# Last two groups of each attention program: all scores of a key tile are issued ahead of the values of the tile before

## The chip, the cores and the metric

The kernel runs on one core of a Trainium2 chip. The metric is the device time of one execution in microseconds. The engines are named as in the profile: PE (TensorE matmuls), PEld (its weight loads), DVE (VectorE), ACT (ScalarE), POOL (GpSimd) and SP (SyncE, which issues DMAs).

## The reference, cut to what matters

A decoder of six blocks, each followed by a residual sum and a layer norm: causal self attention, cross attention to a context of 1024 rows, a soft mixture of experts, causal self attention, cross attention, and a block that holds a causal self attention and a top-2 mixture of experts. Batch 4, 512 rows, width 256, 16 heads of 16. Attention is

```python
w = jnp.einsum('bhnd,bhmd->bhnm', q, k) * jax.lax.rsqrt(float(D))
w = jax.nn.softmax(w, axis=-1)          # causal in self attention
attn = jnp.einsum('bhnm,bhmd->bhnd', w, v)
```

## The kernel before

The five attentions are built as two programs, `first` (self attention a0, then cross attention c0) and `second` (a1, c1, then a2). The soft mixture of experts stands between them and the routed one behind the second. Stages are separated by a barrier of all engines.

An attention program works on groups: one batch and four of its heads. Program `first` has 32 groups (0 to 31), `second` 48 (0 to 47). A group of cross attention has 8 key tiles of 128 keys and all 512 queries; a group of self attention has 4 key tiles, and tile t takes only queries from 128·t on (widths 512, 384, 256, 128). The last two groups are thus cross attention in `first` (30, 31) and causal in `second` (46, 47).

What a group goes through:

- `unit`: scores with queries on the partitions, only to get each row's maximum (DVE). The units of group n+2 are shared out over the steps of group n. The last two groups of a program therefore have none to issue: these are the groups "without maximum scores".
- `chain`: six small DVE steps that split the maximum into three bf16 rows; `shift`: four small matmuls (L1254) and an ACT copy (L1368) that bring it to `shift_T`. Chain and shift of group n+1 happen within group n.
- `scores (t, p)`: scores with keys on the partitions, for key tile t and two of the four heads (p is 0 or 1). PE: two products (L1213), four small mask products in a causal group (L1219), two products that add the shift (L1223). Each fills two PSUM banks. ACT then takes two exponentials (L1357) into `probs`.
- `values t`: PE multiplies tile t's `probs` with `v_aug` into PSUM bank 6 (L1235). It waits for the exponentials of (t, 1). `probs` has two buffers, so ACT's exponentials of tile t wait for the values of tile t-2.
- `drain`: ACT copies bank 6 to `o_sum` when a group's last values are in (L1364); the next group's `values 0` waits for it. `turn`: PE transposes `o_sum` (L1245), DVE normalises it (L1477, L1480).

The order of work is one list, `plan`, written by `attention_plan`. Every engine walks the same list and does the events that are its own, so the order of events in the list is the order of instructions on each engine. The plan's events take PSUM banks in turn out of seven (`SHARED_BANKS`), two for a `scores`; an event may start when the reader of the event seven banks before has read (`wait_bank`). In groups 30, 31, 46 and 47 the plan holds no other products, loads or stores: only scores, values, and one turn, one drain, one `v_aug` addition and, in the first of the two, six chain steps and one shift.

Before the change a step of every group is: scores (t, 0), values t-1, scores (t, 1). In step 0 the last values and the drain of the group before take the place of values t-1; in step 1 the turn follows the values; in the last step the shift comes just ahead of scores (t, 1).

Of the kernel before, what the change touches and what calls it, by code (L numbers as in the profile page):

```python
# [726 lines left out]
def attention_plan(layers, pieces, contexts):  # L727

    slots = [layer for layer in layers for _ in range(BATCH)]
    groups = GROUPS * len(slots)
    plan = []

    def layer_of(n):
        return slots[n // GROUPS]

    def share(stream, done, total):  # L740

        while stream and stream[0][1] * total < done * stream[0][2]:
            plan.append(stream.pop(0)[0])

    def stream_of(events):

        whole, at, out = sum(cost for _, cost in events) or 1, 0, []
        for event, cost in events:
            out.append((event, at, whole))
            at += cost  # L750
        return out

    def body(n):
        units, own = [], [(x, COST.get(x[0], 300)) for x in pieces.get(n, ())]
        if 0 <= n + 2 < groups:
            units = stream_of([(("unit", n + 2, u), 1) for u in range(len(layer_of(n + 2).units))])
        if n < 0:
            plan.extend(x for x, _ in own)
            if n == -1:
                plan.extend([("augment", 0, 0), ("vload", 2, 0)])  # L760
                for k in range(SHIFT_STEPS):
                    plan.append(("chain", 0, k))
                    share(units, k + 1, SHIFT_STEPS)
                plan.append(("shift", 0, 0))
            plan.extend(x[0] for x in units)
            return
        if n == groups:
            last = layer_of(n - 1).key_tiles - 1
            plan.extend([("values", n - 1, last), ("drain", n - 1, 0), ("turn", n - 1, 0)])
            plan.extend(x for x, _ in own)  # L770
            return
        layer, own = layer_of(n), stream_of(own)
        steps = layer.key_tiles
        for t in range(steps):
            plan.append(("scores", n, (t, 0)))
            share(units, 2 * t + 1, 2 * steps)
            if t:
                plan.append(("values", n, t - 1))
            elif n:
                plan.extend([("values", n - 1, layer_of(n - 1).key_tiles - 1), ("drain", n - 1, 0)])  # L780
            if t == 1:
                if n:
                    plan.append(("turn", n - 1, 0))
                if n + 1 < groups:
                    plan.append(("augment", n + 1, 0))
                if n + 3 < groups:
                    plan.append(("vload", n + 3, 0))
                if NB <= n + 3 < groups:
                    plan.append(("load", n + 3, 0))
            if t == steps - 1 and n + 1 < groups:  # L790
                plan.append(("shift", n + 1, 0))
            plan.append(("scores", n, (t, 1)))
            share(units, 2 * t + 2, 2 * steps)
            if n + 1 < groups and t < 3:
                plan.extend([("chain", n + 1, 2 * t), ("chain", n + 1, 2 * t + 1)])
            share(own, t + 1, steps)
        assert not units and not own

    for n in range(-3, groups + 1):
        for event in contexts.get(n, ()):  # L800
            plan.append(event)
        body(n)
    return slots, plan
# [1540 lines left out]
```

How the kernel before makes its waits and increments, by code:

```python
def wait_for(eng, sem, count):  # L50
    if isinstance(count, int) and count <= 0:
        return
    eng.wait_ge(sem, count)
# [70 lines left out]
        @block.gpsimd  # L125
        def _(pool):
            for t in (c.ident, c.ident_bf, c.mask_qk, tri_kq):
                pool.memset(t[:, :], 0.0).then_inc(filled, 1)
            pool.memset(chosen[:, :, :], 0.0).then_inc(filled, 1)
            pool.memset(c.eps[:, :], LN_EPS).then_inc(c.made, 1)
            pool.wait_ge(filled, 5)
            for t in (c.ident, c.ident_bf):
                pool.affine_select(out=t[:, :], in_=t[:, :], compare_op=ALU.not_equal, fill=1.0, base=0,
                                   pattern=[[-1, P]], channel_multiplier=1).then_inc(c.made, 1)
# [3 lines left out]
                               base=0, pattern=[[1, P]], channel_multiplier=-1).then_inc(c.made, 1)  # L138
            for i in range(6):
                if i:
                    pool.wait_ge(filled, 5 + 2 * i)
                for p in range(2):
                    pool.affine_select(out=chosen[:, p, :], in_=chosen[:, p, :], compare_op=ALU.not_equal, fill=1.0,
# [3 lines left out]
        @block.vector  # L149
        def _(v):
            v.wait_ge(c.made, 5)
            for dst, src in ((c.pick, c.ident_bf), (c.mask_kq, tri_kq)):
                for own in (slice(0, 64), slice(64, P)):
                    for x in range(2):
# [1 line left out]
            v.wait_ge(filled, 17)  # L156
            v.tensor_copy(c.choose[:, :, :], chosen[:, :, :]).then_inc(c.made, 1)
            v.wait_ge(c.made, CONSTANTS)
```

## Time and profile before

| | |
|---|---|
| time, median of 3 | 2954.07 us (2953.14 to 2954.84) |
| the profiled execution's own time | 2954.8 us |
| its span | 2953.1 us |
| PE busy | 2536.9 us (86%) |
| ACT busy | 1340.6 us (45%) |
| DVE busy | 1502.1 us (51%) |
| groups 30 and 31, from values to values | 24.12 and 23.80 us |
| groups 46 and 47 | 10.92 and 11.07 us |
| mean granted TensorE clock | 0.933 of full speed |

The span is the time from the first to the last recorded instruction of the one profiled execution; its own time is what the run reports. Starts below are in microseconds from the span's start. Groups 30 and 31 lie at 737 to 785 us, groups 46 and 47 at 2430 to 2452 us.

### The profile page before, as it was taken

To read this page: it belongs to the slowest core of one execution; us is meant where nothing else is said; L and a number is where in the kernel's file an instruction comes from. 1 tells how busy PE (TensorE), PEld (TensorE's weight loads), DVE (VectorE), ACT (ScalarE), POOL (GpSimd) and SP (SyncE) were. 2 spreads that over 40 slices of the span, in tenths; PEclk is the share of its full clock that TensorE was granted. 3 is DMA by queue.
4 is the path that set the end of the run, shared out by engine and by line. 5 is a ranking of instruction groups with operands and counts; after the bars stand their busy time and mean duration, and the time that the engine had idled before them with its cause. 6 is when DMAs were issued, how large, how long until landed. Compare 5 with 4: busy or idle time off the path is not lost. (4 is left out here: it accounts for less than half of the span.)

```text
span 2953.1 us, 47417 instructions
## 1 busy us (share of the span) xinstructions
PE 2536.9 (86%) x15793; PEld 1452.1 (49%) x15794; DVE 1502.1 (51%) x4196; ACT 1340.6 (45%) x2886; POOL 456.4 (15%) x719
## 2 busy tenths in 40 slices
PE   6999999999549889997889899898977995399991
PEld 3555544444224456675555544343434654267761
DVE  2555877888044500024544588777735663222224
ACT  3655467766444422111445457565664552022220
POOL 4233211110200000000122212212023001400004
PEclk8999999999969999998899999999998996599996
DMA  6544533321000022114633433232322325501113
GB/s 207 165 138 139 132 87 93 75 59 43 6 12 1 1 91 91 60 47 151 182 105 122 133 97 90 58 92 63 78 68 75 108 66 189 176 31 32 32 32 91
DMA packets 153825, 259.89 MB, mean 88 GB/s; under 512 B 22712, under 2 KB 96704, under 8 KB 149440
## 3 DMA queue, kind: packets, MB, share of 16 engines
q1 hardware_dynamic: 150544, 248.81, 28.8%
q0 software_dynamic: 3072, 8.39, 0.9%
q8 instruction: 120, 1.97, 0.3%
q14 instruction: 89, 0.73, 0.1%
HBM read 180.71 MB, written 81.53 MB: 89 GB/s over the span
## 5 line engine op out<-in xcount | busy, mean ns | idle before, releaser
L1357 ACT ACTIVATE second_p<-psum 128x512 f32<-128x512 f32 (+3 forms) x1024 | 461.9, 522 | 278.9 <-PE psum L1223 275.4
L1357 ACT ACTIVATE first_p<-psum 128x512 f32<-128x512 f32 (+3 forms) x768 | 365.8, 548 | 171.5 <-PE psum L1223 168.5
L1431 DVE TENSOR_REDUCE second_max_parts<-psum 128x1 f32<-128x512 f32 x512 | 321.5, 682 | 67.7 <-PE psum L1200 66.5
L1431 DVE TENSOR_REDUCE first_max_parts<-psum 128x1 f32<-128x512 f32 x512 | 322.2, 682 | 57.4 <-PE psum L1200 55.6
L1427 DVE CUSTOM_DVE_ANT_0 second_masked<-psum,mask_qk 128x384 f32<-128x384 f32 (+3 forms) x512 | 229.2, 488 | 194.5 <-PE psum L1200 169.8
L1213 PE MATMUL psum<-second_q,second_k 64*128 64x512 f32 (+3 forms) x1024 | 226.1, 437 | 42.8 <-DVE second_max_parts L1431 27.1
L1235 PE MATMUL psum<-second_p,second_v_aug 128*32 128x512 f32 (+3 forms) x2048 | 238.6, 538 | 8.4 <-ACT second_p L1357 8.1
L1200 PE MATMUL psum<-second_k,second_q 64*128 64x512 f32 (+3 forms) x1024 | 201.9, 391 | 27.9 <-DMA second_k<-a_k_parts 15.6
L1213 PEld LDWEIGHTS psum<-second_q,second_k 64*128 64x128 f32 x1024 | 98.1, 187 | 231.3 <-issue 84.0
L1223 PE MATMUL psum<-second_shift_T,choose 64*128 64x512 f32 (+3 forms) x1024 | 197.6, 381 | 0.0
L1235 PE MATMUL psum<-first_p,first_v_aug 128*32 128x512 f32 (+3 forms) x1536 | 184.1, 551 | 11.6 <-ACT first_p L1357 11.6
L1427 DVE CUSTOM_DVE_ANT_0 first_masked<-psum,mask_qk 128x128 f32<-128x128 f32 (+3 forms) x256 | 114.5, 488 | 132.4 <-PE psum L1200 115.2
L2035 ACT ACTIVATE routed_rows_kept<-psum,routed_bias 128x128 f32<-128x128 f32 x312 | 84.7, 382 | 212.1 <-PE psum L1976 212.1
L1213 PE MATMUL psum<-first_q,first_k 64*128 64x512 f32 (+3 forms) x768 | 171.5, 443 | 2.4 <-DVE first_max_parts L1431 1.4
L1200 PE MATMUL psum<-first_k,first_q 64*128 64x512 f32 (+3 forms) x768 | 154.1, 401 | 21.1 <-DMA first_k<-a_k_parts 9.9
L1223 PE MATMUL psum<-first_shift_T,choose 64*128 64x512 f32 (+3 forms) x768 | 148.3, 382 | 0.0
L1213 PEld LDWEIGHTS psum<-first_q,first_k 64*128 64x128 f32 x768 | 72.1, 184 | 153.4 <-ACT first_p L1357 72.2
L1200 PEld LDWEIGHTS psum<-second_k,second_q 64*128 64x128 f32 x1024 | 103.7, 193 | 81.7 <-issue 47.5
L1966 PE MATMUL psum<-routed_up,routed_rows_T 128*128 x312 | 143.2, 602 | 0.3 <-issue 0.3
L1985 PE MATMUL psum<-routed_down,routed_rows_kept 128*128 x624 | 141.1, 379 | 0.0
L1219 PE MATMUL psum<-mask_kq,pick 64*128 64x64 f32 (+1 forms) x1536 | 135.9, 255 | 0.0
L1219 PEld LDWEIGHTS psum<-mask_kq,pick 64*128 64x128 f32 x1536 | 133.6, 190 | 4.1
(317 smaller groups left out, 3800.4 us busy)
## 6 DMA issues: line engine op xcount, KB each, us to landing
first_k<-c_k_parts SPq DMA_DIRECT2D x64, 256.0 KB, 4.7
second_q<-a_q_parts SPq DMA_DIRECT2D x128, 128.0 KB, 2.9
second_k<-a_k_parts SPq DMA_DIRECT2D x128, 128.0 KB, 2.9
second_k<-c_k_parts SPq DMA_DIRECT2D x64, 256.0 KB, 4.6
first_q<-a_q_parts SPq DMA_DIRECT2D x64, 128.0 KB, 2.9
first_k<-a_k_parts SPq DMA_DIRECT2D x64, 128.0 KB, 2.9
c_k_parts<-first_held SPq DMA_DIRECT2D x16, 512.0 KB, 3.1
first_q<-c_q_parts SPq DMA_DIRECT2D x64, 128.0 KB, 4.5
```

The lines of the kernel that those rows point to most:

```text
L1200: ins = pe.matmul(bank_of(event, h)[:, 0:width], qs[r][own, p, qt * P:(qt + 1) * P], keys_of(n)[own, p, k0:k0 + width], start=True, stop=True)
L1213: pe.matmul(bank_of(event, h)[:, q0:SEQ], keys_of(n)[own, p, t * P:(t + 1) * P], qs[r][own, p, q0:SEQ], start=True, stop=False)
L1219: pe.matmul(bank_of(event, h)[:, q0:q0 + 64 * (x + 1)], c.pick[own, x, :], c.mask_kq[own, x, 0:64 * (x + 1)], start=False, stop=False)
L1223: filled(pe.matmul(bank_of(event, h)[:, q0:SEQ], c.choose[own, p, :], shift_T[n % 2][own, q0:SEQ], start=False, stop=True), event)
L1235: ins = pe.matmul(c.psum[32 * j:32 * j + 32, PV_BANK, q0:SEQ], v_aug[n % 2][:, t, j, :], probs[at % 2][:, j, q0:SEQ], start=t == 0, stop=t ...
L1357: evacuated(act.activation(probs[tile % 2][:, 2 * h + p, q0:SEQ], bank[:, q0:SEQ], ACT.Exp, scale=scale), event)
L1427: evacuated(v.tensor_tensor_reduce(masked[:, done % 2, 0:width], bank[:, 0:width], c.mask_qk[:, SEQ - width:SEQ], 1.0, LEAST, ALU.add, ALU ...
L1431: evacuated(v.reduce_max(max_parts[n % 2][:, h, p, qt, k0 // BANK:k0 // BANK + 1], bank[:, 0:width], axis=AX_X), event)
L1966: ins = pe.matmul(c.psum[:, UP_BANK + h, :], rows_T[r][:, k, :], up[:, bass.ds(e, 1), k, h * BANK:(h + 1) * BANK].rearrange("p o n -> p (o ...
L1985: ins = pe.matmul(c.psum[:, DOWN_BANK + r, 0:D], hidden[r][:, m, :], down[:, bass.ds(e, 1), m, :].rearrange("p o n -> p (o n)"), start=m = ...
L2035: act.activation(hidden[r][:, m, :], c.psum[:, TURN_BANK + m // PER, m % PER * P:(m % PER + 1) * P], ACT.Gelu, bias=bias[:, bass.ds(e * HM ...
```

## The change

It concerns the plan alone. In the last two groups of each program (n + 2 >= groups) both `scores` of a tile are put into the plan ahead of `values t-1` (in step 0 ahead of the last values and the drain of the group before, in step 1 ahead of the turn). The shift of the next group stays between the two scores of the last step, and comes with them ahead of the values of tile t-1. The other groups, the work of each event and its buffers stay as they are. Banks are handed out by the plan's order, so within these groups they change with it.

```diff
--- before.py
+++ after.py
@@ -773,6 +773,10 @@
         steps = layer.key_tiles
         for t in range(steps):
             plan.append(("scores", n, (t, 0)))
+            if n + 2 >= groups:
+                if t == steps - 1 and n + 1 < groups:
+                    plan.append(("shift", n + 1, 0))
+                plan.append(("scores", n, (t, 1)))
             share(units, 2 * t + 1, 2 * steps)
             if t:
                 plan.append(("values", n, t - 1))
@@ -787,9 +791,10 @@
                     plan.append(("vload", n + 3, 0))
                 if NB <= n + 3 < groups:
                     plan.append(("load", n + 3, 0))
-            if t == steps - 1 and n + 1 < groups:
-                plan.append(("shift", n + 1, 0))
-            plan.append(("scores", n, (t, 1)))
+            if n + 2 < groups:
+                if t == steps - 1:
+                    plan.append(("shift", n + 1, 0))
+                plan.append(("scores", n, (t, 1)))
             share(units, 2 * t + 2, 2 * steps)
             if n + 1 < groups and t < 3:
                 plan.extend([("chain", n + 1, 2 * t), ("chain", n + 1, 2 * t + 1)])
```

## Rows read from the trace of the kernel before

**Rows 1.** The page, part 1: busy us (share of the span) and instructions of each engine.

```profile
PE 2536.9 (86%) x15793; PEld 1452.1 (49%) x15794; DVE 1502.1 (51%) x4196; ACT 1340.6 (45%) x2886; POOL 456.4 (15%) x719
```

**Rows 2.** Windows of the four groups: stretch, length, busy us of each engine, granted clock, DMA.

```profile
737.28:761.40 24.12, 18.75 (x136) 7.21 (x136) 2.72 (x13) 17.79 (x35) 9.27 (x20) 1.00 0.00 1
761.40:785.20 23.80, 17.69 (x128) 6.72 (x128) 0.68 (x2) 17.08 (x33) 0.00 (x0) 1.00 0.00 1
2429.91:2440.83 10.92, 9.08 (x106) 5.63 (x104) 3.56 (x12) 6.75 (x19) 0.73 (x1) 1.00 0.01 3
2440.83:2451.90 11.07, 8.79 (x101) 5.44 (x101) 0.68 (x2) 6.58 (x19) 0.00 (x0) 1.00 0.00 0
```

**Rows 3.** Timeline inside group 30: start us, length, engine, line, names, count, idle before.

```profile
746.57 1.07 PE L1235 MATMUL psum<-first_p,first_v_aug 128*32 128x512 f32 x8 [0.70 <-ACT first_p L1357]
...
747.57 0.50 PE L1213 MATMUL psum<-first_q,first_k 64*128 64x512 f32 x2
...
748.13 0.39 PE L1213 MATMUL psum<-first_q,first_k 64*128 64x512 f32 x2
...
748.33 2.06 ACT L1357 ACTIVATE first_p<-psum 128x512 f32<-128x512 f32 x4 [0.83 <-PE psum L1223]
...
748.36 0.40 PE L1223 MATMUL psum<-first_shift_T,choose 64*128 64x512 f32 x2
...
749.47 1.06 PE L1235 MATMUL psum<-first_p,first_v_aug 128*32 128x512 f32 x8 [0.71 <-ACT first_p L1357]
```

**Rows 4.** Timeline, PE where group 30 begins, and its turn.

```profile
736.70 0.42 PE L1223 MATMUL psum<-first_shift_T,choose 64*128 64x512 f32 x2
...
737.28 1.06 PE L1235 MATMUL psum<-first_p,first_v_aug 128*32 128x512 f32 x8 [0.16 <-ACT first_p L1357]
...
741.17 0.66 PE L1245 MATMUL psum<-ident,first_o_sum 128*128 128x128 f32 x4
...
741.76 0.50 PE L1213 MATMUL psum<-first_q,first_k 64*128 64x512 f32 x2
```

**Rows 5.** Timeline of the causal groups 45 to 46: PE, ACT and DVE.

```profile
2430.39 0.45 PE L1223 MATMUL psum<-second_shift_T,choose 64*128 64x512 f32 x2
...
2430.76 0.42 PE L1235 MATMUL psum<-second_p,second_v_aug 128*32 128x128 f32 x8
...
2430.93 1.09 ACT L1357 ACTIVATE second_p<-psum 128x512 f32<-128x512 f32 x2 [0.67 <-PE psum L1223]
...
2431.12 0.50 PE L1213 MATMUL psum<-second_q,second_k 64*128 64x512 f32 x2
...
2434.53 0.66 PE L1245 MATMUL psum<-ident,second_o_sum 128*128 128x128 f32 x4
...
2435.12 0.45 PE L1213 MATMUL psum<-second_q,second_k 64*128 64x384 f32 x2
...
2435.80 0.28 PE L1213 MATMUL psum<-second_q,second_k 64*128 64x256 f32 x2
...
2436.53 0.20 DVE L1468 CAST second_shift<-second_rest 128x16 bf16<-128x16 f32 x1
...
2436.92 0.85 PE L1235 MATMUL psum<-second_p,second_v_aug 128*32 128x384 f32 x8 [0.50 <-ACT second_p L1357]
...
2437.71 0.39 PE L1213 MATMUL psum<-second_q,second_k 64*128 64x256 f32 x2
...
2438.27 0.22 PE L1213 MATMUL psum<-second_q,second_k 64*128 64x128 f32 x2
...
2439.75 0.40 PE L1254 MATMUL psum<-ident_bf,second_shift 128*128 128x128 bf16 x4
...
2440.07 0.33 PE L1213 MATMUL psum<-second_q,second_k 64*128 64x128 f32 x2
```

**Rows 6.** Windows of both tails, from the last turn until the last product is in.

```profile
786.99:794.96 7.97, 5.70 (x28) 4.21 (x28) 2.12 (x5) 1.19 (x2) 0.00 (x0) 1.00 0.00 1
2453.04:2465.19 12.15, 9.88 (x28) 6.79 (x28) 1.37 (x3) 1.19 (x2) 0.00 (x0) 0.58 0.00 0
```

## The prediction

> **What bounds the kernel now.** I first read the page's busy times: PE is busy for 86% of the span, ACT for 45% [rows 1]. That average says nothing of the four groups touched, so I cut them out as windows. PE works 18.75 of 24.12 us in group 30, 17.69 of 23.80 in group 31, 9.08 of 10.92 and 8.79 of 11.07 in groups 46 and 47, at full granted clock, with no DMA to speak of; ACT is busy for 17.79, 17.08, 6.75 and 6.58 us [rows 2]. Neither engine fills the time: they wait for each other. The timeline shows how. In a step of group 30 PE starts values at 746.57, scores (t,1) at 747.57, the next tile's (t+1,0) at 748.13, and then sits until 749.47. ACT starts at 748.33, when the first bank of (t,1) is full, and takes four exponentials in 2.06 us: (t,1), then (t+1,0). Values t can start only after the first two, 1.03 us, and about 0.11 us for the signal: 749.47. ACT runs dry at 750.39, because (t+1,1) stands in PE's queue behind those values [rows 3]. The cycle is 1.03 (two exponentials) + 0.11 + 1.00 (values) + 0.76 (scores until a bank is full) = 2.90 us, and ACT idles 0.83 of it. It is a ring of waits, not an engine at its limit.
>
> **The change, part by part.** No instruction is added or removed. Scores (t,1) come ahead of values t-1, so ACT has all four heads of the next tile waiting when it finishes one. The ring is cut: values t still wait for their own exponentials, but the next ones no longer wait for these values. Three things could set the step then.
>
> - ACT: 2.06 us for four exponentials [rows 3].
> - PE: values 1.00, scores (t,0) 0.56, from scores (t,1) to its shift product 0.23 (748.13 to 748.36) [rows 3], and from there to the next values. In this step that last gap is a wait. Where values follow without one it is 2430.39 to 2430.76, 0.37 us, also for 512 columns [rows 5]; I take 0.38. Sum 2.17 us.
> - Banks: a step takes four of seven, so scores (t+1,1) wait for a bank that the first exponential of tile t frees. That is early in ACT's turn. Likewise exponentials of t+1 wait for values t-1, over 0.5 us before.
>
> So PE sets the step, narrowly: 2.17 us against 2.90. PE between values and next values cannot be faster than the rows show unless the 0.15 us beyond the usual 0.23 between products is hidden.
> The Trainium skill (TensorE: Matmul & The Clock Gate, Part 1, "Architectural detail") says that PE's queue pulls weight loads ahead of running matmuls. By it that 0.15 us could be hidden and the step would be ACT's 2.06; the row at 2430.76, which follows scores with nothing to wait for, does not show it.
>
> **Group 30**, counted from its first values (those of group 29). These start at 736.70 + 0.23 + 0.23 + 0.38 = 737.54 and not 737.28, as scores (0,1) now precede them: 0.26 lost [rows 4]. ACT's run of four started at 736.14 and ends at 738.2; scores (0,1) add 1.03 and the drain 0.60, so values 0 start 0.11 after 739.84, at +2.41. Then values 1.00, turn 0.59 (741.17 to 741.76) [rows 4], scores 0.56 + 0.23 + 0.38: values 1 at +5.17. Four steps of 2.17: values 5 at +13.85. The last step holds the shift, 0.32 (2439.75 to 2440.07) [rows 5], and about 0.1 for the products after it: values 6 at +16.44, values 7 at +18.61. Before: 24.12.
> **Group 31** is the same to +13.85; values 6 at +16.02. No scores are left to hide the end: the last exponentials start at 13.85 + 1.00 + 0.76 = 15.61, end at 17.67, values 7 start at +17.78. Before: 23.80.
> Program `first`: 47.92 - (0.26 + 18.61 + 17.78) = 11.3 us less. The tail behind it is the same chain as before.
>
> **Groups 46 and 47**, counted from scores (0,0), 2429.91 in the windows [rows 2]. ACT starts at +1.02, takes 1.09 and 1.03 for 512 columns and 0.60 for the drain: +3.74, values 0 at +3.85. PE would be ready at about +3.5 (scores (0,0) 0.77, scores (0,1) 0.50 + 0.38, the old group's values 0.36, then 0.68 for 384 columns, and the same with the switch [rows 5]). Values 1.00 and turn 0.59 (2434.53 to 2435.12) lead to scores (2,0) at +5.44, (2,1) at +6.00, values 1 at +6.6; these take 0.79 (2436.92 to 2437.71), scores (3,0) about 0.5 (a little under the 0.56 of 2437.71 to 2438.27), the shift 0.32, scores (3,1) up to the values 0.6, values 2 about 0.57 (between 0.79 for 384 columns and 0.36 for 128, 2430.76 to 2431.12): the next group's scores start at +9.37 [rows 5]. Before 10.92: 1.5 us less. Group 47 has no shift (values 2 at +8.45), and its last exponentials end at about +9.0: values 3 at +9.1 against 11.07, 2.0 less. Together 3.5 us.
>
> **What else moves.** The turn now comes after both scores of step 1, and DVE runs the last four chain steps behind it. They end 2.20 us after the turn starts (2434.53 to 2436.73 [rows 5]), so at about +7.05 in group 46; the shift is due at +7.87. Cover 0.8 us, in group 30 over 8 us; without it the next group would start late by the difference. The drain falls behind two more exponentials; that is in the sums. In the last step of the first group of each pair, the shift copy on ACT ends about 0.2 us before PE wants it: nothing. POOL's `v_aug` addition for the next group has a group's time. No DMA is passed. Whatever follows starts behind a barrier and moves up as a whole.
>
> **Sum.** 11.3 + 3.5 = 14.8 us. The profiled execution took 2954.8 us (span 2953.1, some 1.7 around it) and would take 2940.0; the median of 2954.07 becomes 2939.3. A difference under 0.2% (5.9 us) is about what a measurement of this kernel cannot tell from none.
>
> **Rivals.**
> - **Hidden switch, ACT the bound.** The step is 2.06: 0.11 less in some 11 steps, 1.2 us: 2938.1. For it: only 0.1 us separates the two. Against: the row of 0.37.
> - **Banks.** If scores (t+1,1) were in effect let go only after tile t's last exponential, values would start 0.11 + 0.23 + 0.38 = 0.72 us after it, the next scores be full 1.76 us later, and a step be 2.48: 0.31 us more in 13 steps, 4 us: 2943.3. Against: the bank order gives it back with the first exponential; the four readers count up one by one.
> - **The ring closes elsewhere** (late chain, ACT waiting for `probs`), so that half of the gain is left: 7 us, 2947; under 5.9 us it would read as no change.
> - **Clock.** The tail of `second` takes 12.15 us at a mean clock of 0.58, the same work in `first` 7.97 us at 1.00 [rows 6]. The full level is 2.4 GHz, the lower 1.2. In `second` PE was 8.79 of 11.07 us busy ahead of its tail, in `first` 17.69 of 23.80, so the busy share ahead does not explain which tail is slow. Either can flip: 4.2 us less (2935.1), or, if `first`'s tail falls, 4.2 more (2943.5).
> The Trainium skill (same page, "What's actually happening") calls the gate's observation free-running, so that the outcome varies by run; the two tails agree with that, though the three runs lie within 1.7 us.
> - **Slower.** TensorE falls to its lower level inside groups 30 and 31. At half clock a step of 2.17 becomes about 4.1, 1.2 more than before and 1.9 more than forecast. From 8 of the 16 steps on the gain is gone, from 11 on it reads as slower; with all 16, 14.8 - 16 · 1.9 = -15.6: 2969.7. Against: the windows are at 1.00 with more idle than will be left [rows 2].
>
> **Chances.** Forecast (gain 12.5 to 17) 0.67, among it the hidden switch with 0.15; banks 0.08; clock better 0.10, clock worse 0.06; half the gain 0.07, a third of it under 5.9; slower 0.02. The range reaches from the better clock, with the hidden switch (2933.9), to the banks and the worse clock (2943.5): 2934 to 2944. Faster 0.95, same 0.03, slower 0.02.
>
> **What the profile after would show.** In groups 30 and 31 values 2.17 us apart and not 2.90, PE with nearly no idle, ACT with about 0.1 us idle in each four exponentials; windows near 18.6 and 17.8 us from values to values; 9.4 and 9.1 us for groups 46 and 47; PE's idle there ahead of values 0 and the last values alone. Steps of 2.06 mean the switch is hidden, 2.48 banks. The prediction is wrong if something not in these lists binds the step, if the tails' clock flips, or if the chain is late for the shift of group 47.

## The result and the profile after

The changed kernel takes 2937.76 us (median of 6 runs, 2933.41 to 2940.80), the kernel before 2953.61 us in its 6 (2951.75 to 2955.45): 15.9 us less. The ratio is 0.9946, with a 95% interval of 0.9933 to 0.9958. Forecast were 2939.3 us and 14.8 us less. The profiled execution took 2938.45 us.

The page's first part, where the change does not show: PE's share is 86% as in [rows 1], and its busy time is 3 us less.

```profile
span 2936.7 us, 47418 instructions
...
PE 2533.8 (86%) x15793; PEld 1452.9 (49%) x15794; DVE 1502.1 (51%) x4196; ACT 1340.6 (46%) x2886; POOL 456.7 (16%) x719
```

The four groups do show it. Windows of the same stretches as in [rows 2], with the same columns (length, then busy us of PE, PEld, DVE, ACT and POOL):

```profile
740.18:758.54 18.36, 18.19 (x139) 7.25 (x137) 2.35 (x13) 17.38 (x35) 9.27 (x20) 1.00 0.01 1
758.54:776.05 17.51, 16.56 (x126) 6.43 (x124) 0.68 (x2) 16.61 (x33) 0.00 (x0) 1.00 0.00 1
2422.07:2431.35 9.28, 8.88 (x108) 5.66 (x106) 3.05 (x12) 6.96 (x20) 0.73 (x1) 1.00 0.00 0
2431.35:2440.20 8.85, 8.44 (x104) 5.37 (x100) 0.68 (x2) 6.13 (x17) 0.00 (x0) 1.00 0.01 2
```

Groups 30 and 31 take 18.36 and 17.51 us and not 24.12 and 23.80, groups 46 and 47 9.28 and 8.85 and not 10.92 and 11.07. PE is busy for 18.19 of the 18.36 us.

The timeline inside group 30, the rows that answer to [rows 3] (lines from L1200 on have moved by 5):

```profile
747.41 1.07 PE L1240 MATMUL psum<-first_p,first_v_aug 128*32 128x512 f32 x8
...
748.41 0.49 PE L1218 MATMUL psum<-first_q,first_k 64*128 64x512 f32 x2
...
748.98 0.40 PE L1218 MATMUL psum<-first_q,first_k 64*128 64x512 f32 x2
...
749.21 0.40 PE L1228 MATMUL psum<-first_shift_T,choose 64*128 64x512 f32 x2
...
749.54 1.06 PE L1240 MATMUL psum<-first_p,first_v_aug 128*32 128x512 f32 x8
...
745.94 5.36 ACT L1362 ACTIVATE first_p<-psum 128x512 f32<-128x512 f32 x10
```

Values start at 747.41 and 749.54, 2.13 us apart (2.90 before), with no wait noted ahead of them. ACT runs through ten exponentials in 5.36 us without a gap that this view shows (it joins what lies less than 0.15 us apart). Scores (t,1) at 748.98 now come ahead of the values at 749.54.

In group 46 the timeline shows the two places where something could have been late:

```profile
2425.78 1.06 PE L1240 MATMUL psum<-second_p,second_v_aug 128*32 128x512 f32 x8 [0.40 <-ACT second_o_sum L1369]
...
2428.77 0.20 DVE L1473 CAST second_shift<-second_rest 128x16 bf16<-128x16 f32 x1
...
2429.86 0.40 PE L1259 MATMUL psum<-ident_bf,second_shift 128*128 128x128 bf16 x4
```

Values 0 wait 0.40 us for the drain (at +3.71 in the group; forecast +3.85). The last chain step ends at 2428.97, and the shift starts at 2429.86: 0.89 us of cover, where the forecast had 0.8.

The tail behind group 47, to be held against the second row of [rows 6]:

```profile
2441.35:2450.78 9.43, 7.17 (x28) 5.29 (x28) 1.37 (x3) 1.19 (x2) 0.00 (x0) 0.82 0.00 0
```

It takes 9.43 us at a mean granted clock of 0.82 instead of 12.15 at 0.58. The first eight output products there still took 3.43 us, the second eight 1.99. The tail behind group 31 takes 7.97 us at 1.00, as in [rows 6].

### The profile page after: what moved, and what is told of

Its sections match the earlier page's. It is cut to its first block and busy times, and to the rows that moved or that the text cites. A ratio compares the mean times of both kernels' runs of the same rounds, so it can differ in the third digit from the quotient of the medians.

```text
span 2936.7 us, 47418 instructions
## 1 busy us (share of the span) xinstructions
PE 2533.8 (86%) x15793; PEld 1452.9 (49%) x15794; DVE 1502.1 (51%) x4196; ACT 1340.6 (46%) x2886; POOL 456.7 (16%) x719
## 5 line engine op out<-in xcount | busy, mean ns | idle before, releaser
L1205 PE MATMUL psum<-first_k,first_q 64*128 64x512 f32 (+3 forms) x768 | 153.7, 400 | 22.0 <-DMA first_k<-a_k_parts 10.3
```

Of the source, the lines that this page charges most:

```text
L1205: ins = pe.matmul(bank_of(event, h)[:, 0:width], qs[r][own, p, qt * P:(qt + 1) * P], keys_of(n)[own, p, k0:k0 + width], start=True, stop=True)
```

## The experiments

The first four kernels ran on one chip (kernel before: 2958.51 us, median of 19), the next four on the same one in a second series (2956.67, 15 runs), the last two on another (2954.56, 17 runs). A ratio is that of the kernel to the kernel before in the same series, with its 95% interval.

### The order in program `first` alone

```diff
-            if n + 2 >= groups:
+            if n + 2 >= groups and not layer.causal:
...
-            if n + 2 < groups:
-                if t == steps - 1:
+            if n + 2 < groups or layer.causal:
+                if t == steps - 1 and n + 1 < groups:
```

> The new order in program first alone (groups 30 and 31, cross attention). Theory (the gain is the sum of rings cut in each of the four groups, and nothing downstream gives any of it back or adds to it): from values to values 18.4 and 17.5 us in groups 30 and 31 against 24.12 and 23.80 before, so with 0.2 us lost at the first values 11.8 us less than before; groups 46 and 47 at 10.92 and 11.07 as before. Rival (the clock in the tails made part of the gain): the time differs from that sum by 4 us or more while the four groups measure as said.

2948.07 us, ratio 0.9967 (0.9956 to 0.9978): between 6.5 and 13.0 us less by the interval; expected were 11.8. Windows of groups 30 and 31:

```profile
738.75:757.06 18.31, 18.13 (x138) 7.24 (x136) 2.32 (x13) 17.37 (x35) 9.27 (x20) 1.00 0.01 1
757.06:774.58 17.52, 16.56 (x126) 6.42 (x125) 0.68 (x2) 16.62 (x33) 0.00 (x0) 1.00 0.00 1
```

18.31 and 17.52 us, as in the whole change.

### The order in program `second` alone

```diff
-            if n + 2 >= groups:
+            if n + 2 >= groups and layer.causal:
...
-            if n + 2 < groups:
-                if t == steps - 1:
+            if n + 2 < groups or not layer.causal:
+                if t == steps - 1 and n + 1 < groups:
```

> The new order in program second alone (groups 46 and 47, causal). Theory: 9.28 us from scores to scores in group 46 and about 8.8 from scores to last values in group 47, against 10.92 and 11.07: 3.9 us less than before, groups 30 and 31 as before. With the run of the other program alone the two gains add up to that of the whole change, 15.8. Rival (the two halves interact, by the clock or by what runs between): the sum misses 15.8 by more than 4 us.

2950.96 us, ratio 0.9978 (0.9969 to 0.9986): 4.1 to 9.2 us less. The expected 3.9 lies just outside. The windows of both tails, cut as in [rows 6]:

```profile
789.95:801.92 11.97, 9.70 (x28) 6.77 (x28) 2.13 (x5) 1.19 (x2) 0.00 (x0) 0.59 0.00 1
2457.15:2465.13 7.98, 5.71 (x28) 4.21 (x28) 1.37 (x3) 1.19 (x2) 0.00 (x0) 1.00 0.00 0
```

The tail of `second` has the full clock throughout, 7.98 us against 12.15 in [rows 6]. The tail of `first`, behind groups in the old order, went the other way: 11.97 us at 0.59 against 7.97 at 1.00. The two nearly cancel, and this execution (2956.61 us) was the slowest of the kernel's twelve, so the profile does not tell where the median's gain above 3.9 us comes from. The sum of the two halves by their ratios, 9.8 + 6.5 = 16.3 us, misses neither 15.8 nor the whole change by more than noise.

### Less work for ACT in the changed kernel

```diff
-  evacuated(act.activation(probs[tile % 2][:, 2 * h + p, q0:SEQ], bank[:, q0:SEQ], ...
+  end = SEQ // 2 if h and n + 2 >= NGT and not layer.causal else SEQ
+  evacuated(act.activation(probs[tile % 2][:, 2 * h + p, q0:end], bank[:, q0:end], ...
```

> The changed kernel, and in groups 30 and 31 the exponentials of two of the four heads of a tile do only 256 of 512 columns (the other columns of probs stay as they were, so part of the softmax is left out). ACT has about 0.45 us less per step. Theory (PE sets the step of 2.12): the distance of values stays 2.12 us, ACT only idles more; the ends move, since the drain and the last exponentials come earlier, 1.0 to 1.5 us in all. Rival (ACT sets the step): it falls to PE's floor, which the rival puts at 2.02 or below, 0.1 us or more in each of 11 steps.

2939.70 us, ratio 0.9941 (0.9926 to 0.9957). Timeline of group 30:

```profile
747.29 1.06 PE L1240 MATMUL psum<-first_p,first_v_aug 128*32 128x512 f32 x8
...
749.10 1.64 ACT L1363 ACTIVATE first_p<-psum 128x512 f32<-128x512 f32 x4 [0.48 <-PE psum L1228]
...
749.40 1.06 PE L1240 MATMUL psum<-first_p,first_v_aug 128*32 128x512 f32 x8
```

ACT's four exponentials take 1.64 us, and it now waits 0.48 us for PE; values stay 2.11 us apart. The ends moved by 1.0 us (18.06 and 16.82 us for the two groups). ACT does not set the step.

### Three heads of values in the changed kernel

```diff
+  heads = GH - 1 if n + 2 >= NGT and not layer.causal else GH
-  for j in range(GH):
+  for j in range(heads):
       ins = pe.matmul(c.psum[32 * j:32 * j + 32, PV_BANK, q0:SEQ], ...
```

> The changed kernel, and in groups 30 and 31 the values of the fourth head of a group are not computed (one product of four left out). PE has about 0.25 us less per step. Theory (PE sets the step of 2.12, ACT would allow about 2.0): the step falls to ACT's rate, between 1.96 (four times 0.49) and 2.06, so 1 to 2 us less in the two groups. Rival (ACT already sets the step): 2.12 stays.

2941.78 us, ratio 0.9951 (0.9936 to 0.9965). Timeline of group 30:

```profile
746.35 1.06 PE L1241 MATMUL psum<-first_p,first_v_aug 128*32 128x512 f32 x6
...
747.34 0.50 PE L1218 MATMUL psum<-first_q,first_k 64*128 64x512 f32 x2
...
748.45 1.06 PE L1241 MATMUL psum<-first_p,first_v_aug 128*32 128x512 f32 x6
```

Six records in place of eight, and the next scores still start 0.99 us after the values. The edit took no time off PE, so its premise of 0.25 us was wrong, and the run says nothing on what sets the step. A fourth product that adds nothing (1.00 against 0.99 us) means that the four heads' products, each on its own 32 columns of the array, run side by side.

### Half the columns of values in the changed kernel

```diff
+  end = SEQ // 2 if n + 2 >= NGT and not layer.causal else SEQ
   for j in range(GH):
-      ins = pe.matmul(c.psum[..., PV_BANK, q0:SEQ], v_aug[n % 2][:, t, j, :], probs[at % 2][:, j, q0:SEQ], ...
+      ins = pe.matmul(c.psum[..., PV_BANK, q0:end], v_aug[n % 2][:, t, j, :], probs[at % 2][:, j, q0:end], ...
```

> The changed kernel, and in groups 30 and 31 the values of a tile are computed for 256 of 512 queries, all four heads (half of their output is left out). Leaving out one head had taken nothing off the 1.00 us between values and scores, the heads run side by side; half the columns take about 0.43 us off it (0.57 for 256 columns in the causal group). Theory (PE sets the step of 2.12, with ACT close behind): the step falls, but only to ACT's rate, 1.96 (four times 0.49) to 2.06. Rivals: ACT is the bound already (2.12 stays); something else than ACT stands behind PE (1.7).

2938.77 us, ratio 0.9929 (0.9914 to 0.9944). Timeline of group 30:

```profile
742.60 7.96 ACT L1363 ACTIVATE first_p<-psum 128x512 f32<-128x512 f32 x16
...
745.71 0.64 PE L1241 MATMUL psum<-first_p,first_v_aug 128*32 128x256 f32 x8 [0.21 <-ACT first_p L1363]
...
746.28 0.50 PE L1218 MATMUL psum<-first_q,first_k 64*128 64x512 f32 x2
...
747.67 0.64 PE L1241 MATMUL psum<-first_p,first_v_aug 128*32 128x256 f32 x8 [0.19 <-ACT first_p L1363]
```

Values to scores now 0.57 us. The step is 1.96 us, four times ACT's 0.49, ACT goes through 16 exponentials in 7.96 us, and PE waits for it 0.21 us. With the run of less ACT work this closes the case from both sides: relieving ACT leaves 2.11, relieving PE gives 1.96. PE sets the step, ACT stands 0.16 us behind it.

### Less work for ACT in the kernel before

The edit of the third run, in the old order.

> The kernel before, and in groups 30 and 31 the exponentials of two of a tile's four heads do 256 of 512 columns (part of the softmax is left out). One of the two shortened ones lies between scores (t,1) and values t. Theory (in the order before, a step is a ring of two exponentials, values and scores): the step falls from 2.90 by the 0.22 us that one shortened exponential saves, to 2.68, and not by the 0.44 that ACT saves; in the changed kernel the same edit left the step at 2.12. Rivals: PE bound before as well (2.90 stays), ACT bound (2.46).

2953.07 us, ratio 0.9984 (0.9974 to 0.9993). Timeline of group 30:

```profile
745.95 1.06 PE L1235 MATMUL psum<-first_p,first_v_aug 128*32 128x512 f32 x8 [0.50 <-ACT first_p L1358]
...
747.72 1.64 ACT L1358 ACTIVATE first_p<-psum 128x512 f32<-128x512 f32 x4 [1.06 <-PE psum L1223]
...
748.65 1.06 PE L1235 MATMUL psum<-first_p,first_v_aug 128*32 128x512 f32 x8 [0.49 <-ACT first_p L1358]
...
751.34 1.07 PE L1235 MATMUL psum<-first_p,first_v_aug 128*32 128x512 f32 x8 [0.49 <-ACT first_p L1358]
```

Steps of 2.70 and 2.69 us; the ring had said 2.68, PE as the bound 2.90, ACT as the bound 2.46. ACT waits over a microsecond and PE half of one in each step. The same edit that does nothing in the new order shortens the old one by just the exponential that lies in the ring.

### The changed kernel again

> The changed kernel once more, beside the other runs of this chip. If the gain of the trace (11.8 us in the first program, 3.9 in the second) is all there is: 15 to 16.5 us less than before. If the tails' clock makes part of it, the spread of both kernels' runs should be of the size of the tail's 4 us and the difference up to 4 us off.

2940.80 us against 2956.67, ratio 0.9941 (0.9927 to 0.9954). 15.9 us less in the medians, 17.4 by the ratio. The tail of `first`, which in the first profile of the same kernel had taken 7.97 us at 1.00, is longer here:

```profile
776.75:786.42 9.67, 7.39 (x28) 5.35 (x28) 2.13 (x6) 1.19 (x2) 0.00 (x0) 0.82 0.00 1
```

### The order in every group

```diff
-            if n + 2 >= groups:
+            if n >= 0:
...
-            if n + 2 < groups:
+            if n < 0:
```

> The new order in every group of both programs: the maximum scores (units) of group n+2 then come behind both scores of a tile. Theory: in those groups the units already stand where PE would wait, PE idles there only about 0.25 us per step against 0.70, so the ring costs little and the order brings between 0 and 0.25 us in each of some 200 steps, while a step with units takes 8 of the 7 banks, so that scores now meet banks that DVE holds. I expect between 2925 and 2950 us. Rival (the ring costs as much in every group): 0.7 us a step, over 100 us less.

2927.89 us, ratio 0.9899 (0.9883 to 0.9914), inside the expectation and some 13 us below the changed kernel beside it. From drain to drain the groups go two ways: a plain cross attention group takes 23.12 us instead of 24.43, most causal groups take longer, 12.01 instead of 11.56 or 18.84 instead of 18.56. Why the causal groups lose was not tried. This asked for the next run.

### The order in all cross attention groups and the last two causal ones

```diff
-            if n + 2 >= groups:
+            early = n + 2 >= groups or not layer.causal
+            if early:
...
-            if n + 2 < groups:
+            if not early:
```

> The new order in all cross attention groups and in the last two causal groups. Worked out from the drains of the run with the new order everywhere against the kernel before: cross groups 16 to 29 of program first take 370.2 us instead of 383.6, groups 16 to 31 of program second 477.1 instead of 490.2, while causal groups lose some 0.3 to 0.45 us each (12.01 against 11.56, 18.84 against 18.56). Keeping the first and leaving out the second gives 26 us less than the changed kernel, 42 less than before, some 2914. Rival (the causal groups' loss comes from the banks' order as a whole and stays): 2928 as with all groups.

2911.48 us (2908.45 to 2914.23) against 2954.56, ratio 0.9856 (0.9842 to 0.9871): the fastest kernel of the study, 43 us below the one before. Window of group 28 from drain to drain, first in the kernel before, then here:

```profile
684.07:708.50 24.43, 23.85 (x170) 10.43 (x172) 21.24 (x41) 17.72 (x34) 1.29 (x1) 1.00 0.31 76
```

```profile
672.90:696.00 23.10, 23.04 (x170) 10.25 (x170) 21.53 (x41) 17.50 (x35) 1.30 (x1) 1.00 0.34 81
```

and its timeline:

```profile
686.06 1.07 PE L1241 MATMUL psum<-first_p,first_v_aug 128*32 128x512 f32 x8
...
687.05 0.50 PE L1206 MATMUL psum<-first_k,first_q 64*128 64x512 f32 x2
...
687.59 1.97 DVE L1437 TENSOR_REDUCE first_max_parts<-psum 128x1 f32<-128x512 f32 x3
...
688.33 0.19 PEld L1206 LDWEIGHTS psum<-first_k,first_q 64*128 64x128 f32 x2 [0.29 <-DVE first_max_parts L1437]
...
688.76 1.06 PE L1241 MATMUL psum<-first_p,first_v_aug 128*32 128x512 f32 x8
```

One step in a window, in the same columns:

```profile
686.16:688.87 2.71, 2.71 (x24) 1.21 (x28) 2.57 (x6) 2.07 (x5) 0.00 (x0) 1.00 0.00 0
```

Values are 2.70 us apart. PE is busy for all of the step (23.04 of 23.10 us in the group), DVE for 2.57 us of it, so DVE alone is not the bound. The rows show a ring of both: the unit's product at 687.05 is read by DVE from 687.59 to 688.28 (0.69 us for one maximum); the next unit, whose second bank by the plan is that same bank seven places on, loads its weights at 688.33; values follow at 688.76 and another unit 1.00 behind them, 2.71 us in all. PE's own products fill the same time, and no run relieved PE or DVE in these groups, so which of the two holds the step is not shown. In the old order PE was busy for 23.85 of 24.43 us in group 28 and for 18.75 of 24.12 in group 30: there was far less idle time to win here, and the gain is 1.3 us and not 6.

### The same, but the maximum scores ahead of scores (t,1)

```diff
             plan.append(("scores", n, (t, 0)))
-            if n + 2 >= groups:
+            share(units, 2 * t + 1, 2 * steps)
+            early = n + 2 >= groups or not layer.causal
+            if early:
                 if t == steps - 1 and n + 1 < groups:
                     plan.append(("shift", n + 1, 0))
                 plan.append(("scores", n, (t, 1)))
-            share(units, 2 * t + 1, 2 * steps)
...
-            if n + 2 < groups:
+            if not early:
```

> As the run on cross groups, but the first share of the maximum scores of a step comes ahead of scores (t,1), so that scores (t,1) still precede the values but no longer follow scores (t,0) directly. The last two groups have no such share. If the gain of the cross groups comes from scores (t,1) standing ahead of the values, it stays within 3 us; if it comes from fewer switches between work that waits for DVE and work that waits for ACT, half or more of the 26 us is lost.

2953.72 us (2949.09 to 2966.58), ratio 1.0005 (0.9995 to 1.0015): the time of the kernel before. Groups 30 and 31 keep their gain (18.35 us from drain to drain in group 30), but the groups with maximum scores lose as much: the drain of group 29 comes 13 us later than before, 751.3 against 738.4. Window and timeline of group 28:

```profile
695.30:720.70 25.40, 23.67 (x170) 9.82 (x170) 21.25 (x40) 18.18 (x35) 1.30 (x1) 1.00 0.31 73
```

```profile
706.98 1.06 PE L1241 MATMUL psum<-first_p,first_v_aug 128*32 128x512 f32 x8
...
707.97 0.50 PE L1206 MATMUL psum<-first_k,first_q 64*128 64x512 f32 x2
...
708.51 2.48 DVE L1437 TENSOR_REDUCE first_max_parts<-psum 128x1 f32<-128x512 f32 x4 [0.55 <-PE psum L1206]
...
709.35 0.50 PE L1219 MATMUL psum<-first_q,first_k 64*128 64x512 f32 x2 [0.18 <-DVE first_max_parts L1437]
...
710.01 1.06 PE L1241 MATMUL psum<-first_p,first_v_aug 128*32 128x512 f32 x8
```

25.40 us, a microsecond worse than the kernel before. Scores (t,1) at 709.35 wait for DVE. By the plan their second bank is, seven places on, the first bank of the unit computed right behind the last values (707.97), and DVE reads it only from 708.51 to 709.20. The values behind them on PE wait too: 0.99 us from values to that unit, 1.38 from there to scores (t,1) and 0.66 to the next values are the 3.03 us between values. In the run on cross groups the same read of DVE came ahead of a unit (688.33) that stands behind both scores, and held up neither of them. The first reading, a loss of at most 3 us, has fallen. What the second asked for, half or more of the gain lost, came, but not by its reason: the rows show waits for banks that DVE holds, not switches as such.

## Why the prediction was right

**The ring.** The reading of the 2.90 us as a ring of two exponentials, values and scores stood the test that could have broken it: 2.70 and 2.69 with the shortened exponential, where the ring said 2.68.

**PE sets the new step.** Right, from both sides. The term 2.17 was 0.04 too long: the switch from scores to values takes 0.33 us (749.21 to 749.54) and not the 0.38 I took from the 0.37 of [rows 5], read in a causal group. The rival of a hidden switch (2.06) is refuted as a step: 2.12 to 2.13, though the switch costs 0.10 us over the usual 0.23 and not 0.15. ACT's spare time is 0.16 us a step (2.12 against its 1.96), a little more than the 0.1 forecast.

**Groups 30 and 31.** Forecast 18.61 and 17.78, measured 18.36 and 17.51. Values 5 start at +13.59 and +13.58 and not at +13.85, so the switches up to there, each taken 0.04 to 0.05 us too long, make nearly the whole difference. The start lost 0.22 us: values of group 29 now come 1.36 us after ACT's run begins (738.82 to 740.18) instead of 1.14 (736.14 to 737.28); forecast 0.26. Together 47.92 - 0.22 - 18.36 - 17.51 = 11.8 us (forecast 11.3).

**Groups 46 and 47.** Forecast 9.37 and about 9.1, measured 9.28 and 8.85: 3.9 us (forecast 3.5). The drain did set values 0, but earlier than said: four exponentials in a row bring the drain 1.93 us after the first of them starts (2423.08 to 2425.01 in group 46), where I had added up 1.09 and 1.03.

**Sum.** 15.7 us by the traces of the four groups, 14.8 forecast, 15.9 by the medians. The interval of the ratio is 12.4 to 19.8 us, so that the medians meet the traces within 0.2 us is in part luck.

**The clock of the tails.** The prediction had a flip of a tail's clock among its rivals (0.10 for the better one) and among the signs of being wrong. In the profiles it came in part: the tail of `second` takes 2.7 us less. The twelve profiles, from the last drain of a program until its last product is in, in us:

| kernel | order in `first`: tail | order in `second`: tail |
|---|---|---|
| before | old: 8.6 | old: 12.8 |
| before, less ACT | old: 8.6 | old: 12.6 |
| first alone | new: 8.6 | old: 12.6 |
| second alone | old: 12.6 | new: 8.6 |
| change | new: 8.6 | new: 10.1 |
| change again | new: 10.3 | new: 10.2 |
| three heads | new: 8.6 | new: 10.0 |
| half values | new: 11.0 | new: 10.2 |
| less ACT, all groups, units first | new: 8.6 each | new: 8.6 each |
| cross groups | new: 10.3 | new: 11.3 |

With the old order ahead of it, the clock fell and stayed at its lower level to the end in four tails of six and never fell in two. With the new one it fell for a part in eight of eighteen and not at all in ten. The counts alone would suggest that the order plays a part, but the same kernel has 8.6 and 10.3 in `first`, and `first` kept the full clock twice behind the old order. One profile of a kernel cannot tell the order from chance here, and no run tried it by itself: whether the change has a share in the tails' clock stays open.

In the two profiles compared above, the groups give 15.7 us and the tail of `second` 2.7, and the span is 16.4 shorter. The 2.0 us between are the sum of stretches that the change does not touch: values of group 29 start 2.9 us later (0.22 of that is the change), the stretch from the last drain of `first` to the first of `second` takes 1.4 us more (637.1), what lies behind the last product of `second` 2.0 less (486.0). Over all profiles these two stretches run from 635 to 641 and from 486 to 491 us, and the runs of one kernel on one chip spread over 6 to 11 us (2937.85 to 2943.48, 2950.36 to 2961.68). The interval of the medians holds 15.7 and 18.4 alike.

**Rivals.** Banks: no step of 2.48 us in groups 30 and 31, refuted here; in groups with units waits for banks are real (the last two runs). Half the gain, slower: no sign; the granted clock stayed at 1.00 in all four groups.

## What to carry to other kernels

When two engines idle in the same step, follow the ring of waits and ask which instruction stands in a queue behind a wait it has nothing to do with; moving that one cost 0.22 us here, and the new step can be added up from what the busier engine issues, switches included. What the move is worth in other groups depends on the next reader in line: here the same order gains 6 us a group with no maxima, 1.3 with them (PE is then busy throughout, and units wait for banks that DVE reads), and loses 0.3 to 0.45 in most causal groups. The order among the moved pieces matters as much: one event of another reader between the two scores cost the whole 42 us between the last two runs.

## What the runs showed of the hardware

- Four products on separate 32-column strips of the array, 512 columns each in f32, take 1.00 us to the next scores; three take 0.99. Half the columns take 0.57.
- Exponentials of 128x512 in a row start 0.49 us apart, while the record of one is 0.60 us long; four count as 1.96 and not as 2.4.
- In a tail with little work the granted clock differs between two executions of the same kernel: 7.97 us at 1.00 and 9.67 us at 0.82 for the same stretch. Eight output products took 3.75 us at the lower level and 1.99 at the full one. What decides it was not found.
